# Two powers in place of four on GpSimd, and the row maxima's causal mask added by VectorE

## What is computed

```python
att = einsum('bhqd,bhkd->bhqk', rope(q), rope(k)) / sqrt(16)
att = where(tril, att, -inf)
att = softmax(concat([sink_col, att], -1))[..., 1:]        # 12 heads of 16
h = h + (att @ v) @ W_proj ...                             # on layernorm(h)

xn  = rms_norm(layernorm(h), norm_weight)                  # the experts' input
tok = xn / maximum(sqrt(sum(xn * xn)), 1e-5)
logits = einsum('sd,btd->bst', sl, tok)                    # 64 slots
dispatch_w, combine_w = softmax(logits, -1), softmax(logits, -2)
```

## Time and profile before

| | |
|---|---|
| median of three runs | 3242.63 us (3231.22 to 3243.88) |
| the profiled execution | 3236.77 us, span 3235.0 us |
| mean granted TensorE clock | 0.945 |
| busy, share of the span | TensorE 88%, its weight loads 65%, VectorE 51%, ScalarE 50%, GpSimd 38% |
| main loop, residuals of the first and the last sample | 252.6 and 2748.0 us |

### The profile page before, as it was taken

One profiled execution on the slowest core, in us unless ns is written; L12 is line 12 of the kernel. 1 busy time (PEld: TensorE's weight loads), 2 busy tenths in 40 slices (PEclk: granted clock), 3 DMA queues, 4 the chain that ended last, 5 costly groups with the idle time before them and its releaser, 6 DMA issues. The chain is left out here.

```text
span 3235.0 us, 74217 instructions
## 1 busy us (share of the span) xinstructions
PE 2841.3 (88%) x27010; PEld 2110.1 (65%) x27010; DVE 1649.1 (51%) x5416; ACT 1607.5 (50%) x3234; POOL 1214.2 (38%) x2197
## 2 busy tenths in 40 slices
PE   3079999999999999999999999999999998677765
PEld 3057777777777777777777777777777776343432
DVE  2435556556665655555555556555555554111123
ACT  0036666666666666666666666666666654100000
POOL 2134444444444444444444444444444442000000
PEclk8589999999999999999999999999999998788878
DMA  4233333333333333333333333333333321899979
GB/s 107 44 94 89 89 89 89 89 89 90 92 95 91 95 90 94 90 91 90 93 91 90 93 91 92 90 91 91 89 89 89 89 73 36 220 270 234 250 217 290
DMA packets 368824, 361.31 MB, mean 112 GB/s; under 512 B 32478, under 2 KB 339755, under 8 KB 368204
## 3 DMA queue, kind: packets, MB, share of 16 engines
q1 hardware_dynamic: 344332, 339.13, 40.2%
q10 hardware_dynamic: 24128, 17.42, 1.7%
HBM read 196.51 MB, written 43.25 MB: 74 GB/s over the span
## 5 line engine op out<-in xcount | busy, mean ns | idle before, releaser
L961 DVE TENSOR_REDUCE negmax<-ps 128x1 f32<-128x325 f32 (+2 forms) x2304 | 668.2, 350 | 154.6 <-PE ps L607 147.9
L562 PE MATMUL ps<-window_w,xp 108*98 108x193 f32 x2304 | 505.5, 338 | 107.7 <-ACT xp L814 107.7
L814 ACT ACTIVATE prob<-ps 128x590 f32<-128x590 f32 x768 | 500.8, 660 | 180.2 <-PE ps L630 165.2
L605 PE MATMUL ps<-kst,qst 99*128 99x325 bf16 (+2 forms) x2304 | 397.1, 252 | 22.2 <-DVE negmax L961 22.1
L562 PEld LDWEIGHTS ps<-window_w,xp 108*98 108x98 f32 x2304 | 337.2, 166 | 110.7 <-ACT xp L814 107.8
L1151 POOL TENSOR_TENSOR rot<-by_cos,by_sin 96x324 f32<-96x324 f32 x128 | 111.8, 873 | 684.3 <-DVE by_sin L1054 684.3
L607 PE MATMUL ps<-causal,ident_b 128*128 128x128 bf16 (+1 forms) x2304 | 336.0, 214 | 0.0
L771 PE MATMUL ps<-xt,wqk 97*96 97x324 f32 (+1 forms) x1024 | 320.9, 446 | 1.7 <-ACT xt L814 1.7
L605 PEld LDWEIGHTS ps<-kst,qst 99*128 99x128 bf16 (+1 forms) x2304 | 225.2, 104 | 120.3 <-DVE negmax L961 40.1
L646 PE MATMUL ps<-prob,vaug 128*32 128x324 f32 (+2 forms) x4608 | 285.6, 340 | 0.0
L1041 DVE RECIPROCAL rden<-ps 98x12 f32<-98x12 f32 (+1 forms) x192 | 43.4, 226 | 384.0 <-PE ps L790 383.9
(11 more groups left out here) (184 smaller groups left out, 5884.1 us busy)
## 6 DMA issues: line engine op xcount, KB each, us to landing
w<-in_L_ffn_fc_weight_dram SPq DMA_DIRECT2D x128, 576.0 KB, 13.2
xw<-in_x_dram SPq DMA_DIRECT2D x384, 189.0 KB
qst<-part SPq DMA_DIRECT2D x768, 60.8 KB
kst<-part SPq DMA_DIRECT2D x768, 60.8 KB
h_held<-h_new SPq DMA_DIRECT2D x64, 288.0 KB, 4.3
residual_image<-h SPq DMA_DIRECT2D x64, 147.0 KB
h_i<-residual_image SPq DMA_DIRECT2D x16, 588.0 KB
out_dram<-h_i ACTq DMA_DIRECT2D x32, 294.0 KB
```

The costliest lines, as they stand in the source:

```text
L562: mm = pe.matmul(ps[0:TILE, BK7, half * (D + 1):(half + 1) * (D + 1)], xp[:, q, TILE * half:TILE * (half + 1)], window_w[:, q, :], start=( ...
L605: pe.matmul(ps[0:nq, bk, col:col + keys], qst[i][0:MAX_ROW, h, q0:q0 + nq], kst[i][0:MAX_ROW, h, 0:keys], start=True, stop=False)
L814: return nc.scalar.activation(out_, in_, f, **kw)
L961: last = dve.tensor_reduce(negmax[0:nq, q, h:h + 1], ps[0:nq, bk, col:col + q0 + nq + 1], AX.X, ALU.max, negate=True)
```

## The change

On GpSimd the two square roots of the normalisations become one: alpha = (v (1 + eps) + eps^2)^-1/2, which is a * r, and beta = alpha * max(s * alpha^2, 1e-10)^-1/2. Twelve operations, four of them powers, become seven with two powers. The wait for the sums of squares (`zs_ready`) stands before the fourth operation of the new chain, in the old one before the eighth.

In `scores` the three mask matmuls of a head go, with their weight loads. VectorE's `tensor_reduce` becomes a `tensor_tensor_reduce`: it adds a slice of a new fp32 table `late` (325 columns, 0 and in the last 128 columns the causal table), multiplies by -1, writes the result back over the scores in PSUM and keeps the minimum in `negmax`. The table is made once, by a memset and a copy in the setup. Each query tile takes the slice that puts the causal table on its last columns.

```diff
--- before.py
+++ after.py
@@ -101,6 +101,7 @@
             sink_p = sb("sink_p", [1, PARTS, NH], BF16, layers)
             ident_b = sb("ident_b", [128, 128], BF16, layers)
             causal = sb("causal", [128, 128], BF16, layers)
+            late = sb("late", [128, KEYS], F32, layers)
             cos_t = sb("cos_t", [HALF, T], F32, layers)
             sin_t = sb("sin_t", [HALF, T], F32, layers)
 
@@ -225,6 +226,8 @@
                         dve.tensor_scalar(wp[0:HALF, 1, :], wp[0:HALF, 1, :], rz[0:HALF, 0:1], None, ALU.mult)
                         dve.tensor_copy(ident_b[:], ident[:])
                         dve.tensor_copy(causal[:], causal_f[:])
+                        dve.memset(late[:, 0:KEYS - 128], 0.0)
+                        dve.tensor_copy(late[:, KEYS - 128:KEYS], causal_f[:])
 
                         dve.wait_ge(sums, 1)
                         dve.tensor_tensor(hb[:], ps[:, 0, 0:D], biasb[:], ALU.add)
@@ -348,7 +351,7 @@
                 rstd2 = tmp("rstd2", [128, 3])
                 zss, alpha, beta_t = tmp("zss", [128, 3]), tmp("alpha", [128, 3]), tmp("beta_t", [128, 3])
                 pw = tmp("pw", [128, 3])
-                neg_half, pos_half, neg_one, eps = (tmp(n, [128, 3]) for n in ("neg_half", "pos_half", "neg_one", "eps"))
+                neg_half, eps = (tmp(n, [128, 3]) for n in ("neg_half", "eps"))
                 zero = tmp("zero", [128, 3, NH // 2])
 
                 logit, lexp = tmp("logit", [128, 3, NS]), tmp("lexp", [128, 3, NS])
@@ -437,8 +440,6 @@
                         dve.memset(eps[:], EPS)
                         dve.memset(zero[:], 0.0)
                         dve.memset(per_strip[:], 1.0 / STRIP)
-                        dve.memset(pos_half[:], 0.5)
-                        dve.memset(neg_one[:], -1.0)
                         for t in (lmax, lsum, mrest, rstd2):
                             dve.memset(t[:], 1.0)
                         dve.drain()
@@ -602,10 +603,8 @@
                         for q, bk, col in ((2, bank, 0), (0, bank + 1, 0), (1, bank + 1, QTILES[0][1] + 1)):
                             q0, nq = QTILES[q]
                             keys = q0 + nq + 1
-                            pe.matmul(ps[0:nq, bk, col:col + keys], qst[i][0:MAX_ROW, h, q0:q0 + nq],
-                                      kst[i][0:MAX_ROW, h, 0:keys], start=True, stop=False)
-                            mm = pe.matmul(ps[0:nq, bk, col + q0 + 1:col + keys], ident_b[:, 0:nq], causal[:, 0:nq],
-                                           start=False, stop=True)
+                            mm = pe.matmul(ps[0:nq, bk, col:col + keys], qst[i][0:MAX_ROW, h, q0:q0 + nq],
+                                           kst[i][0:MAX_ROW, h, 0:keys], start=True, stop=True)
                         mm.then_inc(s_mm.sem, 1)
 
                     def scores_t(b, i, h):
@@ -958,8 +957,11 @@
                                 s_mm.wait(dve, b, h + 1)
                                 for q, bk, col in ((2, bank, 0), (0, bank + 1, 0), (1, bank + 1, QTILES[0][1] + 1)):
                                     q0, nq = QTILES[q]
-                                    last = dve.tensor_reduce(negmax[0:nq, q, h:h + 1], ps[0:nq, bk, col:col + q0 + nq + 1],
-                                                             AX.X, ALU.max, negate=True)
+                                    keys, gone = q0 + nq + 1, KEYS - 129 - q0
+                                    last = dve.tensor_tensor_reduce(
+                                        out=ps[0:nq, bk, col:col + keys], in0=ps[0:nq, bk, col:col + keys],
+                                        in1=late[0:nq, gone:gone + keys], scale=-1.0, scalar=-MASKED, op0=ALU.add, op1=ALU.min,
+                                        accum_out=negmax[0:nq, q, h:h + 1])
                                 last.then_inc(max_ready.sem, 1)
                             if moe and h == 1:
 
@@ -1100,26 +1102,17 @@
 
                             ln2_ready.wait(pool, b - 1)
                             dp_ready.wait(pool, b - 2)
-                            var = mv2[:, :, 1]
-                            pool.tensor_tensor(alpha[:], var, eps[:], ALU.add)
+                            pool.tensor_scalar(alpha[:], mv2[:, :, 1], 1.0 + EPS, EPS * EPS, ALU.mult, ALU.add)
                             power(alpha[:], alpha[:], neg_half[:])
                             pool.drain()
                             pool.tensor_tensor(pw[:], alpha[:], alpha[:], ALU.mult)
                             pool.drain()
-                            pool.tensor_tensor(pw[:], var, pw[:], ALU.mult)
+
+                            zs_ready.wait(pool, b - 1, apart=True)
+                            pool.tensor_tensor(pw[:], zss[:], pw[:], ALU.mult)
                             pool.drain()
-                            pool.tensor_scalar(pw[:], pw[:], EPS, 1.0, ALU.add, ALU.mult)
+                            pool.tensor_scalar(pw[:], pw[:], 1e-10, 0.0, ALU.max, ALU.add)
                             power(pw[:], pw[:], neg_half[:])
-                            pool.drain()
-                            pool.tensor_tensor(alpha[:], alpha[:], pw[:], ALU.mult)
-
-                            zs_ready.wait(pool, b - 1, apart=True)
-                            power(pw[:], zss[:], pos_half[:])
-                            pool.drain()
-                            pool.tensor_tensor(pw[:], pw[:], alpha[:], ALU.mult)
-                            pool.drain()
-                            pool.tensor_scalar(pw[:], pw[:], 1e-5, 0.0, ALU.max, ALU.add)
-                            power(pw[:], pw[:], neg_one[:])
                             pool.drain()
                             pool.tensor_tensor(beta_t[:], pw[:], alpha[:], ALU.mult).then_inc(beta_ready.sem, 1)
                         if att:
```

## The result

The changed kernel takes 3151.98 us (3141.75 to 3169.39, four runs) against 3243.26 us: a ratio of 0.974, 95% interval 0.970 to 0.977. Timed again beside later experiments it took 3159.72 us against 3232.29, ratio 0.978 (0.974 to 0.982). The forecast was 3152. The agreement to the microsecond is luck, as will be seen: the loop gave back less than forecast, and an untouched part of the profiled execution was short.

What follows compares the result with a forecast made beforehand. It took TensorE, tied to other engines at three places, to bound each step. A gain of 1.37 us x 64 = 88 us from 3236.8 gave 3149; set between the profiled execution and the median, 3152 us, range 3105 to 3250.

Steps and rivals of the forecast that it cites:

- GpSimd's chain is the hold at head 8: TensorE waits at head 8 for GpSimd's maxima parts; two fewer powers and three fewer small operations make them ready by 1532.17.
- The size of TensorE's wait: TensorE's wait at head 8 for GpSimd's parts of the maxima, taken as 1.09 us a step.
- the mark against which every case was held: End of VectorE's first-half work in today's step, 1537.96; the unpaused end 1525.08 + 12p meets it at p = 1.073 us a head.
- the 1.37 forecast: First exp of the attention on ScalarE comes at 1537.15 in place of 1538.52, 1.37 us sooner a step.
- the ceiling of 2.9 us: TensorE, per step: 1.8 us of masks over 12 heads plus the 1.09 us wait at head 8, if nothing else were late.
- VectorE's price, taken as 0.92: VectorE's time for one head's three maxima with the new instruction: 0.92 us, against 0.80 today.
- C: Rival: reading and writing one PSUM bank takes turns on VectorE, 1.48 us a head, 3550 us; chance 0.15.
- B: Rival: accumulator reads or the new instruction's start cost VectorE in line, 0.97 to 1.10 us a head; chance 0.22.
- D: Rival: VectorE stays out of the way, TensorE keeps 1.9 to 2.9 us a step, 3115 to 3050 us; chance 0.09.
- z as 1.24 us: VectorE's z, between its first two heads and heads 2 to 9, taken as 1.24 us as today.
- The chain through the dispatch maximum: VectorE's last heads and dispatch maximum end at 1536.6; ScalarE's dispatch exp follows, its first attention exp 0.53 us later.
- The second half passes the gain through: The step's second half is unchanged work, so the gain of 1.37 us at the first exp passes through whole.

Runs made afterwards that it cites:

- the early maximum: The changed kernel with VectorE's dispatch maximum taken right behind head 10 in place of behind head 11: 3131.9 us, ratio 0.965.

## Why the prediction was right, step by step

- **GpSimd's chain is the hold at head 8, and goes:** right; the powers alone take 0.77 us off. In the changed kernel the parts are ready before TensorE arrives. One step of it was wrong: the changed order does add a wait. GpSimd now waits 23.9/39 = 0.61 us a step for ScalarE's squares, and then for the sixth head's maximum:

```profile
POOL pw L1112 <- ACT lexp L813: 23.9, 39, 0.9
...
1529.38 0.20 POOL L1112 TENSOR_TENSOR pw<-zss,pw 128x3 f32<-128x3 f32 x1 [0.63 <-ACT lexp L813]
1531.65 0.22 POOL L1083 TENSOR_TENSOR mpart<-negmax,zero 128x18 bf16<-128x18 f32 x1 [0.32 <-DVE negmax L961]
1532.72 0.22 POOL L1089 TENSOR_TENSOR mpart<-mrest,mpart 128x18 bf16<-128x18 f32 x1
...
1533.81 0.31 PE L673 MATMUL ps<-ident_b,mpart 68*18 68x68 bf16 x3
```

The parts end at 1532.94, 0.87 us before TensorE needs them, so the wait costs nothing.

- **The size of TensorE's wait:** mis-sized. I took 1.09 us from the one step of the timeline; the mean of the waits is 30.4/38 = 0.80, and it stood in my own rows. The end of VectorE's work at 1537.96, the mark against which every case was held, is late for the same reason: 17.01 us behind its step's residual (1520.95), and 16.76 on the mean of the steps. So 0.25 us of the 1.37 forecast was never there. The new end came 15.54 us behind the residual on the mean, 0.1 us sooner than the forecast's 15.65, and the first exp 1.22 us sooner than before (17.32 to 16.10 behind the residual). The misread step is the error; 1.22 is what the chain gave.
- **Masks, 0.15 us a head on TensorE:** the ceiling of 2.9 us was not reached, as said. With the powers in place they add 38.84 - 38.48 = 0.36 us a step; without them they lose.
- **VectorE's price, taken as 0.92:** 0.96 in a row of heads, 0.92 otherwise. The choice near the one row of the instruction was sound, and the allowance for the write into PSUM fell on the right cause, with 0.02 allowed and 0.04 found for each instruction. The signs given for it were too low: the records are 519, 267 and 400 ns and the reads 138, not 490, 220, 355 and 70. C is excluded by the rate. B did not come true, but by little: 0.96 lies just under its lower edge of 0.97. D is excluded by the period, which is 38.48 and not under 37.6. The estimate from the Trainium skill (VectorE: DVE Perf Modes, the errata section), 1.05 us a head, does not fit the trace's 0.96 either.
- **z as 1.24 us:** 0.99, for the overlap shown above. It gives back what the heads cost more, which no term of the sum foresaw.
- **The chain through the dispatch maximum:** right, by the early maximum (0.35 us for 0.39). It ends in TensorE's wait for the first exp, 0.4 us at most.
- **The second half passes the gain through:** nearly. 1.22 us at the first exp became 1.13 in the period, and 38.48 is not the 38.2 that was to show it. I had no term for the clock, and none was needed at 1.00; but the mask alone shows what it can cost. It was named among the signs, and had no rival and no chance of its own.
- **The total:** the mechanism was right, and the hit is luck. 72 us come from the loop against 88, and 12.6 us from the draw of the expert part, which happen to add to the forecast for the profiled execution. The repetition, 73 us under the kernel before beside it, has the size that the loop explains.

## What to carry to other kernels

Work taken from an engine pays only behind the wait that holds it: the same mask move is worth 0.36 us a step once the wait is gone and costs 1.1 us while it stands (71 us over 64 steps). Take a wait's size from its mean over the steps, not from the step whose timeline you read. When an instruction is used only for its accumulator, look where its unwanted elementwise result goes, and order the engine that is now full by what waits on each result.

## What was not expected of the hardware

- TensorE's granted clock fell to its lower level for some microseconds at or behind a wait of 1.3 to 1.9 us in 50 of 61 steps, in a stretch otherwise dense, and stayed at 1.00 in the kernel before, with waits of up to 1.1 us. Matmuls put in front of the wait brought it back to 1.00, and 65 us with it. What decides in which step it falls is not shown: of two steps with the same wait of 1.39 us one kept 1.00 and one did not.
- Writing the elementwise result back to the PSUM bank it was read from rather than to SBUF costs VectorE about 0.04 us an instruction here, and the accumulator read's record grows from 0.07 to 0.13 us.
- VectorE's z, with both inputs in SBUF, took longer by just the time for which it overlapped GpSimd's subtraction: 0.44, 0.36 and 0.17 us. No run moved the two apart on purpose.
